# Rows of the experts' region in DRAM: 576 bytes apart in place of 528

## The chip, the cores and the metric

The kernel runs on one core of one Trainium2 chip. The metric is the time of one execution on the device in microseconds (us), the median of several runs. A core has five engines with an instruction stream each: TensorE (PE; its weight loads are listed as PEld), VectorE (DVE), ScalarE (ACT), GpSimd (POOL) and SyncE (SP), which here only issues DMAs. Sixteen DMA engines move data between DRAM and the on-chip memory.

## The reference

256 images of 128 channels and 7 x 7 places (12544 tokens of 128 numbers) pass four layers: window attention with a layer norm, a group-norm attention, and then twice an attention followed by a mixture of experts. The mixtures are what the change touches:

```python
scores = jnp.einsum('bne,ex->bnx', x, Wg) + bg
topk_vals, topk_idx = jax.lax.top_k(scores, TOP_K)      # TOP_K = 2 of 8 experts
gates = jax.nn.softmax(topk_vals, axis=-1)
h = jax.nn.gelu(jnp.einsum('bne,xeh->bnxh', x, W1) + b1, approximate=False)
expert_out = jnp.einsum('bnxh,xhe->bnxe', h, W2) + b2
out = jnp.einsum('bnx,bnxe->bne', combine, expert_out)  # combine: the two gates at the two experts
```

The second mixture has the same form with a hidden size of 512 in place of 192 and the tanh form of gelu. All numbers are fp32.

## The kernel before

The program runs stages one after another, with a barrier of all engines between two: window attention, group-norm attention, **dispatch 2** (the token attention of layer 2, and the sorting of tokens by expert), **blocks 2** (the experts' products), a combination of the two results of each token, **dispatch 3** (the attention of layer 3, and again the sorting), **blocks 3**, and a final combination with the store. The same class `Dispatch` sorts in both dispatch stages.

**The region.** `expert_rows` is a tensor in DRAM of 8 x 13312 + 512 rows, 13312 rows for each expert and 512 spare ones. A row is one token for one expert: its 128 normalised numbers (C = 128), then four more: the token's number (column C), its first expert (C + 1), and its two gates (C + 2, C + 3). A row is so 132 numbers, 528 bytes, and rows lie without a gap.

**Dispatch.** Tokens go in 98 tiles of 128, in chunks of 4 tiles (`CHUNKS_D2`, 25 chunks) or 3 (`CHUNKS_D3`, 33). A chunk's rows are put together in one of three tiles `row` (`NR = 3`): ACT writes the normalised numbers (L1375) and the first two columns (L1396, L1398), DVE the gates (L1497, L1499). DVE computes for each token the two places in the region (`pos`), and `scatter` on POOL sends each tile of 128 rows twice, one indirect DMA (L1565) for each of the two experts: 2 x 98 DMAs in a stage. At the start of the stage DVE runs `prepare`, which waits for eight loads of constants (L1405 and after), the last of them `d_pad` (L1258), a tile of 4 x 128 empty rows. When the places of all tokens are known, SP runs `pads`: it puts 512 empty rows behind the last token of each of the eight experts (L1277), waits for all of them (L1281), and the stage ends.

**Blocks.** `blocks_phase` goes over 56 blocks of 512 rows. For block b SP issues the load of the rows, `moe_xb<-expert_rows` (L2524), and then that of the expert's weights, `moe_w<-moe_split` (L2528). Three blocks can be loaded ahead; before the load of rows SP waits until the rows of block b-3 have been used (L2522), and before that of weights until the output `ys` of block b-3 is there (L2527). SP's queue is in order, so the rows of block b+1 are issued after the weights of block b. PE turns the 4 x 128 rows (L2539), multiplies by the first weights in chunks of the hidden size (L2551 to L2553; K is 2 chunks in blocks 2 and 4 in blocks 3), and by the second ones two chunks later (L2563 to L2565). POOL sends the results, rows of 128 numbers, 512 bytes, to `expert_out` (L2688, four indirect DMAs for each block).

The load of rows is one DMA whose destination is a tile of 128 partitions x 4 rows; in the trace it is 512 packets of one row, 32 on each of the 16 DMA engines. The empty rows are written in packets of one row in the same way.

Of the kernel before, what the change touches and what calls it, by code (L numbers as in the profile page):

```python
# [23 lines left out]
C = 128  # L24
# [19 lines left out]
REGION = 13 * 1024  # L44
assert REGION >= TOKENS + BLOCK
NBLK = (2 * TOKENS + EXPERTS * (BLOCK - 1)) // BLOCK
ROW = C + 4
FAR = 4.0 * TOKENS
EXP_SET = "natural_log_exp_and_others"

# [1135 lines left out]
class Dispatch:  # L1186
# [7 lines left out]
    def __init__(self, nc, sh, sb, sem, kind, e, wsplit, rows_dram, chunks, xt, small, joint=False):  # L1194
# [12 lines left out]
        self.upto8, self.steps, self.blocks = sb("upto8", [C, EXPERTS * EXPERTS]), sb("steps", [C, STEPS]), sb("blocks", [C, NBLK])  # L1207
        self.pad = sb("pad", [C, BLOCK // C, ROW])
        self.raw = [sb(f"raw{i}", [C, e.half]) for i in range(2)]
        self.wh, self.wl = [sb(f"wh{i}", [C, e.half], F32R) for i in range(2)], [sb(f"wl{i}", [C, e.half]) for i in range(2)]  # L1210
        self.st, self.mv = sb("dst", [C, QUAD, 6]), [sb(f"mv{i}", [C, QUAD, 2]) for i in range(2)]
        self.rs = [sb(f"drs{i}", [C, self.wide]) for i in range(2)]
        self.row = [sb(f"row{i}", [C, self.wide, ROW]) for i in range(self.NR)]
        self.lg = sb("lg", [C, self.wide, EXPERTS])
# [69 lines left out]

    def centre_gate(self, pe):
        pe.matmul(self.small[:, 0:EXPERTS], self.sh.centre_w[:, :], self.wg[:, :], start=True, stop=True).then_inc(self.centred, 1)
        pe.wait_ge(self.ready, 6)

    def turn(self, pe, q):
        c, t0, nt, o = self.quads[q]  # L1290
# [111 lines left out]
    def prepare(self, dve):  # L1402
        dve.memset(self.count[0][:, :], 0.0).then_inc(self.count_done, 1)
        dve.memset(self.base16[:, :], 0.0).then_inc(self.ready, 1)
        dve.wait_ge(self.loaded, 16 * 8)  # L1405
        dve.wait_ge(self.ready, 1)
        dve.tensor_copy(self.base16[0:1, :], self.base8[0:1, :]).then_inc(self.ready, 1)
        dve.tensor_copy(self.below[:, :], self.below_f[:, :]).then_inc(self.ready, 1)
        dve.tensor_copy(self.ones[:, :], self.ones_f[:, :]).then_inc(self.ready, 1)
        dve.wait_ge(self.centred, 1)  # L1410
        dve.tensor_copy(self.wgc[:, C:], self.small[:, 0:EXPERTS]).then_inc(self.ready, 1)
        dve.tensor_copy(self.wgc[:, 0:C], self.sh.centre_w[:, :]).then_inc(self.ready, 1)
# [143 lines left out]

    def scatter(self, pool, c, tiles=None):
        nt, j = self.chunks[c][1], c % self.NR
        pool.wait_ge(self.pos_done, c + 1)
        pool.wait_ge(self.normed, self.last_quad[c] + 1)  # L1560
        pool.wait_ge(self.col_done, c + 1)
        pool.wait_ge(self.named, 2 * c + 2)
        for i in range(nt) if tiles is None else tiles:
            for k in range(2):
                pool.indirect_dma_start(out=self.rows_dram, out_offset=bass.IndirectOffsetOnAxis(ap=self.pos[j][:, i, k:k + 1], axis=0),  # L1565
                                        in_=self.row[j][:, i, :], in_offset=None).then_inc(self.scattered[j], 16)
# [898 lines left out]
def blocks_phase(nc, sh, kind, e, func, wsplit, rows_dram, y_dram):  # L2465
# [8 lines left out]
    with ExitStack() as ctx:  # L2474
        def sb(name, shape, dt=F32):
            return ctx.enter_context(nc.sbuf_tensor(f"{kind}_{name}", shape, dt))
# [11 lines left out]
        w = [sb(f"w{i}", [C, e.width], F32R) for i in range(NW)]  # L2488
        xb = [sb(f"xb{i}", [C, S, ROW]) for i in range(NX)]
        xh, xl = [sb(f"xh{i}", [C, BLOCK], F32R) for i in range(2)], [sb(f"xl{i}", [C, BLOCK], F32R) for i in range(2)]  # L2490
# [329 lines left out]
def build(nc, a, out):  # L2820

    sh = Shared()
    sh.inputs = a
    rows_dram = nc.dram_tensor("expert_rows", (EXPERTS * REGION + BLOCK, ROW), F32, kind="Internal").ap()
    y_dram = nc.dram_tensor("expert_out", (2 * TOKENS, C), F32, kind="Internal").ap()
# [37 lines left out]
def constants():  # L2863
# [15 lines left out]
    one["c_blocks"] = np.tile(np.arange(NBLK, dtype=f), (C, 1))  # L2879
    pad = np.zeros((C, BLOCK // C, ROW), f)  # L2880
    pad[:, :, C] = FAR
# [51 lines left out]
```

## Time and profile before

| | |
|---|---|
| three runs | 2543.06, 2551.14, 2556.58 us; median 2551.14 |
| the profiled execution | 2569.39 us, its span 2567.6 us |
| busy: PE, DVE, ACT, POOL | 1885.7, 1682.2, 1394.9, 1398.4 us |
| DMA | 233.59 MB, 169830 packets |
| granted TensorE clock, mean | 0.836 |

The profile shows one execution of the program. Busy times are those of instructions that compute; an engine's idle time is put down to what ended it, an engine with a line or a DMA. The share of DMA is the mean over the 16 DMA engines. The profiled execution took 0.7% longer than the median of the three runs.

### The profile page before, as it was taken

Reading aid. Unit: us, or ns where it says so; the run is one execution under the profiler, and the core shown is the slowest. Engines: PE = TensorE matmul, PEld = TensorE weight load, DVE = VectorE, ACT = ScalarE, POOL = GpSimd, SP = SyncE. Lnnn points to the kernel's source line nnn. Section 1 sums busy time; section 2 is a strip of 40 time slices with the busy share of each in tenths; the row PEclk is TensorE's granted clock in tenths of the full one; section 3 lists DMA queues with packets and bytes.
Section 4 is the critical chain, followed back from the end, with each engine's and each line's share of the span. In section 5 each row is a group of like instructions: output and inputs, shape, how many; then the busy total and the mean of one; then the engine's idle time right before and its main releaser. Section 6 shows DMA issues by size and latency. Waiting matters only on the chain. (4 is left out here: it accounts for less than half of the span.)

```text
span 2567.6 us, 52818 instructions
## 1 busy us (share of the span) xinstructions
PE 1885.7 (73%) x16257; PEld 1299.3 (51%) x16257; DVE 1682.2 (66%) x4786; ACT 1394.9 (54%) x3150; POOL 1398.4 (54%) x1485
## 2 busy tenths in 40 slices
PE   7999998986546561677767478777777629999993
PEld 4555556764434451445544334444444427777772
DVE  5888886865434442455555458888888637887773
ACT  5777764645333431444444067777777417777760
POOL 4555560102434345356556637878787736776665
PEclk9999998988766755788888578979888659999995
DMA  5000000002101001555544511111110036777757
GB/s 115 3 0 0 0 1 1 0 16 81 51 29 35 26 33 57 151 146 147 142 137 136 209 21 66 51 47 52 47 62 25 29 122 214 227 230 230 228 170 300
DMA packets 169830, 233.59 MB, mean 91 GB/s; under 512 B 60032, under 2 KB 131957, under 8 KB 162190
## 3 DMA queue, kind: packets, MB, share of 16 engines
q1 hardware_dynamic: 142446, 172.32, 22.4%
q0 software_dynamic: 26880, 52.27, 6.1%
q10 hardware_dynamic: 288, 6.42, 0.6%
q8 instruction: 99, 1.62, 0.3%
q14 instruction: 117, 0.96, 0.1%
HBM read 155.37 MB, written 79.23 MB: 91 GB/s over the span
## 5 line engine op out<-in xcount | busy, mean ns | idle before, releaser
L2688 POOL DMA_INDIRECT expert_out<-moe_yr,moe_to x448 | 475.4, 1061 | 341.7 <-DVE moe_yr L2667 223.9
L1565 POOL DMA_INDIRECT expert_rows<-d_row,d_pos x392 | 381.1, 972 | 355.7 <-issue 163.5
L2603 ACT ACTIVATE moe_ah<-moe_hps,moe_w 128x512 f32<-128x512 f32 (+1 forms) x336 | 229.9, 684 | 256.5 <-PE moe_hps L2553 181.0
L2644 DVE TENSOR_TENSOR moe_hl<-moe_ah,moe_hh 128x512 fp32r<-128x512 f32 (+1 forms) x336 | 232.9, 698 | 171.4 <-ACT moe_hh L2608 108.9
L1782 PE MATMUL scales_ptps<-ident,scales_pr 113*128 113x113 f32 x512 | 110.0, 319 | 124.1 <-DVE scales_sc L1880 81.7
L2551 PE MATMUL moe_hps<-moe_xh,moe_w 128*128 128x512 f32 (+1 forms) x336 | 142.4, 424 | 48.3 <-DMA moe_w<-moe_split 32.4
L550 POOL TENSOR_TENSOR window_pr<-window_pr,window_rc 113x392 f32<-113x392 f32 x128 | 109.1, 852 | 106.8 <-DVE window_rc L494 106.7
L1782 PEld LDWEIGHTS scales_ptps<-ident,scales_pr 113*128 113x128 f32 x512 | 67.9, 163 | 179.2 <-DVE scales_sc L1880 95.3
L2563 PE MATMUL moe_yps<-moe_hh,moe_w 128*128 128x512 f32 (+1 forms) x336 | 152.5, 454 | 2.7 <-issue 0.9
L2539 PE MATMUL moe_xps<-ident,moe_xb 128*128 128x128 f32 x448 | 79.3, 306 | 95.5 <-DMA moe_xb<-expert_rows 91.1
L2564 PE MATMUL moe_yps<-moe_hl,moe_w 128*128 128x512 f32 (+1 forms) x336 | 138.7, 413 | 0.0
L2565 PE MATMUL moe_yps<-moe_hh,moe_w 128*128 128x512 f32 (+1 forms) x336 | 138.4, 412 | 0.0
L2552 PE MATMUL moe_hps<-moe_xl,moe_w 128*128 128x512 f32 (+1 forms) x336 | 137.8, 410 | 0.0
L2553 PE MATMUL moe_hps<-moe_xh,moe_w 128*128 128x512 f32 (+1 forms) x336 | 137.3, 409 | 0.0
L538 POOL TENSOR_TENSOR window_sc<-window_sc,window_mx 113x392 f32<-113x392 f32 x128 | 108.0, 844 | 50.2 <-DVE window_mx L468 49.3
L2539 PEld LDWEIGHTS moe_xps<-ident,moe_xb 128*128 128x128 f32 x448 | 58.6, 155 | 126.6 <-DMA moe_xb<-expert_rows 110.3
L2633 DVE TENSOR_TENSOR moe_xl<-moe_xps,moe_xh 128x512 fp32r<-128x512 f32 x112 | 76.5, 683 | 69.4 <-ACT moe_xh L2596 60.1
L2294 PE MATMUL d_turn<-ident,d_xn 128*128 128x128 f32 x128 | 28.0, 359 | 124.8 <-issue 93.7
L657 ACT ACTIVATE window_pt<-window_ptps 128x452 f32<-128x452 f32 x128 | 69.8, 546 | 90.0 <-PE window_ptps L334 89.9
L2011 POOL TENSOR_TENSOR scales_pr<-scales_pr,scales_fac 113x416 f32<-113x416 f32 x128 | 114.1, 904 | 3.9 <-DVE scales_fac L1918 2.5
L2139 ACT ACTIVATE scales_pt<-scales_ptps 128x452 f32<-128x452 f32 x128 | 69.9, 546 | 83.2 <-PE scales_ptps L1782 83.0
L2608 ACT ACTIVATE moe_hh<-moe_ah 128x512 fp32r<-128x512 f32 (+1 forms) x168 | 106.1, 632 | 5.3
(290 smaller groups left out, 5391.8 us busy)
## 6 DMA issues: line engine op xcount, KB each, us to landing
moe_w<-moe_split SPq DMA_DIRECT2D x56, 1026.5 KB
moe_xb<-expert_rows SPq DMA_DIRECT2D x112, 264.0 KB
moe_w<-moe_split SPq DMA_DIRECT2D x56, 449.5 KB
c_yy<-expert_out SPq DMA_DIRECT2D x28, 448.0 KB
final_yy<-expert_out SPq DMA_DIRECT2D x28, 448.0 KB
expert_out<-moe_yr,moe_to POOLq DMA_INDIRECT x448
X<-in_x SPq DMA_DIRECT2D x32, 196.0 KB
expert_rows<-d_row,d_pos POOLq DMA_INDIRECT x392
```

Of the source, the lines that this page charges most:

```text
L1565: pool.indirect_dma_start(out=self.rows_dram, out_offset=bass.IndirectOffsetOnAxis(ap=self.pos[j][:, i, k:k + 1], axis=0), in_=self.row[j] ...
L1782: last = pe.transpose(ptps[:, hp * R:(hp + 1) * R], pr[at.r][p][:, 2 * hp:2 * hp + 2, :].rearrange("q h k -> q (h k)"), ident[0:R, 0:R])
L2539: last = pe.transpose(xps[:, t * C:(t + 1) * C], xb[b % NX][:, t, 0:C], ident[:, :])
L2551: pe.matmul(out, ww[:, W1H + k * P:W1H + (k + 1) * P], xh[j][:, :], start=True, stop=False)
L2552: pe.matmul(out, ww[:, W1H + k * P:W1H + (k + 1) * P], xl[j][:, :], start=False, stop=False)
L2553: pe.matmul(out, ww[:, W1L + k * P:W1L + (k + 1) * P], xh[j][:, :], start=False, stop=True).then_inc(h_mm, 1)
L2563: pe.matmul(out, ww[0:P, W2H + k * C:W2H + (k + 1) * C], high, start=(k == 0), stop=False)
L2564: pe.matmul(out, ww[0:P, W2H + k * C:W2H + (k + 1) * C], low, start=False, stop=False)
L2565: pe.matmul(out, ww[0:P, W2L + k * C:W2L + (k + 1) * C], high, start=False, stop=(k == K - 1)).then_inc(y_mm, 1)
L2603: act.activation(ah[n % NH][0:P, :], hps[n % 3][0:P, :], func, bias=bias(b, k)[0:P]).then_inc(h_done, 1)
L2644: dve.tensor_tensor(hl[n % NH][0:P, :], ah[n % NH][0:P, :], hh[n % NH][0:P, :].bitcast(F32), ALU.subtract).then_inc(hl_done, 1)
L2688: pool.indirect_dma_start(out=y_dram, out_offset=bass.IndirectOffsetOnAxis(ap=to[j][:, t:t + 1], axis=0), in_=yr[j][:, t, :], in_offset=No ...
```

## The change

`ROW` is 144 in place of 132. Rows of the region, the tiles `row`, `pad` and `xb`, and the constant `c_pad` get 12 more numbers behind the four columns, so each of their transfers grows by one eleventh; a row now starts at a multiple of 576 = 9 x 64 bytes, where it started at a multiple of 528 = 33 x 16 bytes. Nothing reads the 12 numbers. As `scatter` sends whole rows, DVE sets them to zero once for each of the three tiles `row`, and three waits are adapted; `scatter` gets one wait more, once for each chunk.

```diff
-ROW = C + 4
+ROW = C + 16
...
     def centre_gate(self, pe):
         pe.matmul(self.small[:, 0:EXPERTS], self.sh.centre_w[:, :], self.wg[:, :], start=True, stop=True).then_inc(self.centred, 1)
-        pe.wait_ge(self.ready, 6)
+        pe.wait_ge(self.ready, 6 + self.NR)
...
     def prepare(self, dve):
         dve.memset(self.count[0][:, :], 0.0).then_inc(self.count_done, 1)
         dve.memset(self.base16[:, :], 0.0).then_inc(self.ready, 1)
+        for row in self.row:
+            dve.memset(row[:, :, C + 4:], 0.0).then_inc(self.ready, 1)
         dve.wait_ge(self.loaded, 16 * 8)
-        dve.wait_ge(self.ready, 1)
+        dve.wait_ge(self.ready, 1 + self.NR)
...
     def scatter(self, pool, c, tiles=None):
         nt, j = self.chunks[c][1], c % self.NR
+        pool.wait_ge(self.ready, 1 + self.NR)
         pool.wait_ge(self.pos_done, c + 1)
```

The only instructions that are added are on DVE, at the start of each dispatch stage. This is DVE's order there in dispatch 2 before (a row is line, operation, output<-input, size):

```order
L2330 MEMSET d_pt 128x392
L1403 MEMSET d_count 128x4
L1404 MEMSET d_base 128x4
L1407 CAST d_base<-d_base 1x8
L1408 CAST d_below<-d_below_f 128x128
```

And this is the same place of the changed kernel, whose lines below L1404 have moved by two and below the scatter by three:

```order
L2333 MEMSET d_pt 128x392
L1403 MEMSET d_count 128x4
L1404 MEMSET d_base 128x4
L1406 MEMSET d_row 128x4x12 x3
L1409 CAST d_base<-d_base 1x8
L1410 CAST d_below<-d_below_f 128x128
```

Three small memsets stand ahead of the cast that waits for the constants; nothing else has moved on any engine.

## Rows read from the trace of the kernel before

**Rows 1.** Busy us (instructions) of each engine by stage, clock, DMA
```profile
590.00:1037.00 447.00, 218.61 (x1549) 175.59 (x1547) 191.86 (x1047) 150.25 (x523) 188.38 (x196) 0.68 0.15 47
1036.00:1412.00 376.00, 269.78 (x1106) 189.98 (x1106) 201.76 (x497) 171.56 (x278) 212.53 (x213) 0.83 0.51 144
1488.00:2104.00 616.00, 431.81 (x5219) 260.59 (x5217) 479.07 (x1509) 414.66 (x1005) 434.56 (x491) 0.80 0.14 46
2104.00:2500.00 396.00, 378.28 (x1788) 296.65 (x1788) 300.12 (x671) 277.74 (x449) 245.79 (x219) 0.99 0.70 221
```
**Rows 2.** Waits in blocks 2 (1036 to 1412): us, times, longest
```profile
PE moe_xps L2539 <- DMA moe_xb<-expert_rows: 70.7, 33, 34.2
PE moe_hps L2551 <- DMA moe_w<-moe_split: 29.7, 25, 2.2
```
**Rows 3.** The same two waits in blocks 3 (2104 to 2503)
```profile
PE moe_xps L2539 <- DMA moe_xb<-expert_rows: 20.4, 1, 20.4
PE moe_hps L2551 <- DMA moe_w<-moe_split: 2.7, 1, 2.7
```
**Rows 4.** Timeline in blocks 2: start us, us, instruction [idle before]
```profile
1236.65 0.34 SPq L2528 DMA_DIRECT2D moe_w<-moe_split  x1
1238.87 0.00 SPq L2524 DMA_DIRECT2D moe_xb<-expert_rows  x1
1240.12 0.47 PE L2551 MATMUL moe_hps<-moe_xh,moe_w 128*96 128x512 f32 x1 [1.34 <-DMA moe_w<-moe_split]
1241.91 0.90 PE L2539 MATMUL moe_xps<-ident,moe_xb 128*128 128x128 f32 x3 [0.86 <-DMA moe_xb<-expert_rows]
```
**Rows 5.** Timeline, end of dispatch 2, and SP's wait for the pads
```profile
1007.61 24.15 SPq L1277 DMA_DIRECT2D expert_rows<-d_pad  x8
...
1009.27 0.96 POOL L1565 DMA_INDIRECT expert_rows<-d_row,d_pos  x1 [0.30 <-issue]
1010.53 0.95 POOL L1565 DMA_INDIRECT expert_rows<-d_row,d_pos  x1 [0.31 <-issue]
1011.79 0.96 POOL L1565 DMA_INDIRECT expert_rows<-d_row,d_pos  x1 [0.30 <-issue]
...
1024.42 0.96 POOL L1565 DMA_INDIRECT expert_rows<-d_row,d_pos  x1 [0.30 <-issue]
...
SPq L1281 <- DMA expert_rows<-d_pad: 2.2, 1, 2.2
```
**Rows 6.** DMA queues (packets, MB, share of 16 engines): 1026:1034, 650:1000, 1060:1400, 2120:2480
```profile
q1 hardware_dynamic: 2112, 1.08, 44.9%
...
q0 software_dynamic: 5120, 10.82, 9.3%
...
q1 hardware_dynamic: 33625, 36.55, 40.2%
...
q1 hardware_dynamic: 34944, 68.72, 62.2%
```
**Rows 7.** Indirect DMAs on POOL, ns min/median/max: rows of 528 and of 512 bytes
```profile
L1565 POOL DMA_INDIRECT expert_rows<-d_row,d_pos x392: 952/959/1280, 621.7 to 2092.4; - x196
L2688 POOL DMA_INDIRECT expert_out<-moe_yr,moe_to x448: 980/984/1459, 1055.2 to 2508.0; - x150
```
**Rows 8.** DVE's start of dispatch 2 and of dispatch 3
```profile
565.64 0.06 DVE L1404 MEMSET d_base<- 128x4 uint32 x1
569.00 0.16 DVE L1407 CAST d_base<-d_base 1x8 bf16<-1x8 f32 x1 [3.29 <-DMA d_pad<-in_c_pad]
...
1472.39 0.11 DVE L1851 MEMSET scales_xn<- 128x24 f32 x2
...
1478.08 0.16 DVE L1407 CAST d_base<-d_base 1x8 bf16<-1x8 f32 x1 [5.31 <-DMA d_pad<-in_c_pad]
```

## The prediction

> **What bounds the kernel now.** I read three views. The windows by stage come first [rows 1]. In both dispatch stages the DMA engines are busy for about a seventh of the time (0.15 and 0.14), in blocks 2 for half (0.51), in blocks 3 for 0.70. In blocks 3 PE is busy 378.28 of 396 us: that stage goes at PE's pace. In blocks 2 it is busy 269.78 of 376, so something else is in the way there. The waits name it second: in blocks 2 PE waits 70.7 us for the rows of a block, 33 times, of which 34.2 are the one wait at the stage's start, and 29.7 us for weights [rows 2]. What is left, 70.7 - 34.2 = 36.5 us in 32 waits, is the only place where transfers of rows hold PE again and again. In blocks 3 there is one wait of each kind, the first block's [rows 3]. The timeline shows what such a wait is made of: SP issues the rows at 1238.87 and PE starts on them at 1241.91, 3.0 us later, having stood for 0.86 [rows 4]. The reader should see that these 3 us are mostly the way to DRAM and back, as the packets of a load take less than 1 us (below). Third, the ends of the dispatch stages. POOL issues its last scatter at 1024.42, but SP's eight pads go from 1007.61 to 1031.76 and it waits 2.2 us more for them [rows 5]. So the stage ends with a DMA of rows, not with the scatters.
>
> **What a packet of a row costs now.** Between 1026 and 1034 the hardware queue carries only pads: 2112 packets, 44.9% of 16 engines over 8 us, so 0.449 x 8 x 16 / 2112 = 27.2 ns for a packet of at most 528 bytes [rows 6]. For the price of 48 more bytes I take the two windows of the blocks stages, where packets differ mostly in size. Blocks 2: 0.402 x 340 x 16 = 2187 us for 33625 packets and 36.55 MB. Blocks 3: 0.622 x 360 x 16 = 3583 us for 34944 packets and 68.72 MB [rows 6]. With a cost for each packet and one for each byte, these two equations give 18.7 ns for a packet and 0.0426 ns for a byte (scale the first to 34944 packets: 2273 us and 37.98 MB; the difference is 1310 us for 30.74 MB). Hence 48 bytes cost 2.0 ns. The bounds: 0, if the transfer goes in units that both lengths fill alike, and 27.2 / 11 = 2.5 ns if all of a packet's time is in its bytes. A load of rows or a pad is 32 packets on each engine, 0.87 us now, so it gets 32 x 2.0 = 0.064 us longer (0 to 0.08).
>
> Does the start at a multiple of 64 bytes give something back? The rows of a pad start at multiples of 16 bytes, most of them off 64, and their mean of 27.2 ns is not above what the fit gives for 528 bytes anywhere in memory, 18.7 + 22.5 = 41 ns with the traffic of the stage in it. The fit cannot exclude that part of these 41 ns is alignment, so it stays as a rival. I take 0 as the gain.
>
> The Trainium skill, "DMA: Bandwidth & Descriptors", section "How a descriptor splits into AXI transactions", has a rule that bears on this: a transfer is cut at multiples of 256 bytes and counted in beats of 32, and one that starts off such a multiple pays for the bytes before its start too. By it 528 bytes at multiples of 16 would cost 17 to 24 beats, 20.5 in the mean (an estimate from that page), and 576 bytes at multiples of 64 cost 18 to 24, 21 in the mean. By the rule the change would then make a packet 2.4% dearer, 0.7 ns or 0.02 us a load, a third of what I take, and the sum below would be +0.8 us; no run here shows single packets by their start yet.
>
> **The change part by part**, against the profiled execution (span 2567.6, time 2569.39 us).
>
> 1. Loads of rows in blocks 2. Each of the 32 waits that are not the first can get 0.064 us longer: 2.0 us. At most all 56 blocks would feel 0.08 us, 4.5 us; at least 0, since a wait for rows is followed by one for weights in 25 cases and may be paid back there. I take 2.0, because PE stands at most of them [rows 2].
> 2. Loads of rows in blocks 3: no wait but the first [rows 3]. What hides them is PE, busy 378 of 396 us, and the three blocks ahead; the row traffic adds 56 x 0.064 = 3.6 us to DMA engines that are busy 277 us of 396. Without this cover it would cost these 3.6 us. Taken: 0.
> 3. The first load of each blocks stage, after which everything waits: 2 x 0.064 = 0.13 us.
> 4. The last pad of each dispatch stage, for which SP waits: 0.13 us. The seven pads ahead are spaced by SP's issue, 24.15 us for seven intervals and the last issue, so about 3.4 us apart, against 0.87 us of packets [rows 5, 6], so they hide their longer packets.
> 5. The scatters: 392 DMAs, each 16 packets of 8 rows. From 650 to 1000 us 5120 packets (half of them the 4-byte signal) take 0.093 x 350 x 16 = 521 us, 203 ns a packet of 8 rows with its signal [rows 6]. They grow to about 219 ns, while POOL issues one each 1.26 us (1009.27, 1010.53, 1011.79 [rows 5]). What sets that pace is POOL's own instruction, and it does not follow the row's length: median 959 ns for 528 bytes and 984 for 512 [rows 7]. Cost 0; without the cover the 16 ns a DMA would come to 196 x 0.016 = 3.1 us in each dispatch.
> 6. The extra wait of each chunk on POOL. Behind it is the scatter of the chunk, and for its landing the writers of the tile wait three chunks later. The value it waits for is reached at the start of the stage. The step from 1009.27 to 1010.53 is the one from a chunk to the next, with four waits in it already, and its idle time is 0.31 us, as inside a chunk, 0.30 [rows 5]. Cost 0; the bound is 0.01 us x 58 chunks = 0.6 us.
> 7. Three memsets on DVE, twice. The nearest row is two memsets of 24 numbers a partition in 0.11 us; three of 48 are about 0.2 to 0.3 us. They run where DVE then stands 3.29 and 5.31 us for the constants [rows 8]. Cost 0; uncovered they are 0.6 us in all. PE's wait for `ready` behind them ends with DVE's last copy, which has not moved.
> 8. The constant `d_pad`, the load that ends this standing, goes from 2112 to 2304 bytes a partition: 192 x 0.0426 = 8 ns for each of 8 packets on an engine, 2 x 0.065 = 0.13 us.
>
> Sum: 2.0 + 0.13 + 0.13 + 0.13 = +2.4 us, bounds 0 and 4.5 + 0.5 + 0.6 + 0.6 = 6.2 us. On 2569.39 that is +0.09%; on the median of 2551.14 it gives 2553.5 us. The three runs of before lie between 2543.06 and 2556.58, 0.5% apart: a difference of less than 0.5%, 12.8 us, cannot be told from none, and this scatter, not the sum, makes the forecast's own range: 2543 to 2564.
>
> **The rivals.**
>
> A, the forecast: extra bytes, nothing back, most of it hidden. 2553.5 us.
>
> B, alignment pays in the blocks stages. In favour: the fit's 41 ns against 27.2 in the quiet window leaves 14 ns a packet that contention or alignment may explain. If all 14 went, a load would be 32 x 14 = 0.45 us shorter, and 32 waits of blocks 2 (1.14 us each in the mean) would give 14.4 us: 2551.1 - 14.4 + 2.4 = 2539 us. Against: the pads, which have the same unaligned starts, show no such part. From 12.8 / 32 = 0.4 us a load on it counts as faster. If the waits for rows vanished altogether (36.5 us), the time would be 2515.
>
> C, the other side: the new pitch collides in DRAM. Rows of one partition in a load lie 128 x 576 = 73728 bytes apart, which is 9 x 8192, before 33 x 2048; the regions of two experts lie 117 x 65536 bytes apart, before 429 x 16384. If whatever spreads addresses over the memory's banks looks at those low bits, the 16 engines, which start together, meet in the same bank. If a packet took twice its 27.2 ns, a load would be 0.87 us longer: 32 x 0.87 = 28 us in blocks 2, 2579 us in all. It decides (over 12.8 us) from 0.4 us a load on, a packet of 40 ns in quiet. For it speaks only the arithmetic; against it, that 9 is odd and no row shows such a collision at 2048 or 16384.
>
> D, the clock. In blocks 2 the granted clock is 0.83 in the mean [rows 1]. A small shift of the stages can change where it falls. A mean 0.02 lower or higher stretches 269.78 us of PE by 2.4%, 6.5 us either way: 2547 or 2560, still within the same.
>
> E, the rule of the skill as written, an arithmetic of beats, is a smaller sum of the same sign, and its chance is in A's.
>
> **How the numbers follow.** A with D around it 0.86; B over 0.5% 0.06; C over 0.5%, with what I have not seen of its kind, 0.08. The predicted time is A's. A's own 2543 to 2564 holds some four fifths of its share; to have 8 in 10 of all, I widen it to 2541 to 2566. Faster 0.06, same 0.86, slower 0.08.
>
> **What would show it.** Right: in quiet stretches with pads alone a packet of 29 to 30 ns; POOL's indirect DMA at 959 ns and 1.26 us apart; the first waits of DVE at 3.3 and 5.3 us; waits for rows in blocks 2 of 36 to 40 us without the first; blocks 3 with no wait but the first. Wrong: a packet of pads under 27 ns or over 40, waits for rows in blocks 2 that fall by half (B) or grow by 15 us or more (C), or a change in a stage that touches no rows.

## The result, and the profile after

The changed kernel takes 2562.56 us in the median of 12 runs (2554.16 to 2576.49), the kernel before 2551.00 us in 12 runs beside them (2541.92 to 2564.1). The ratio is 1.0049, with a 95% interval of 1.0028 to 1.0070: slower by 11.6 us between the medians. (The ratio isn't the quotient of the two medians, which is 1.0045.) A second set of runs of both gave 1.0049 again (1.0026 to 1.0073). The forecast was 2553.5 us, and +2.4 us.

The profiled execution has a span of 2562.5 us, less than the 2567.6 of before: single executions of one program lie up to 22 us apart (2541.92 and 2564.10), so the two spans can't be compared. Stages are compared below over several profiles.

The windows by stage of the changed kernel, laid to the same places of the stages as [rows 1] (busy us and instructions of PE, PEld, DVE, ACT, POOL; clock; DMA share; GB/s):

```profile
585.00:1032.00 447.00, 219.69 (x1571) 176.89 (x1571) 193.72 (x1050) 151.88 (x530) 187.93 (x196) 0.69 0.15 50
1031.50:1407.50 376.00, 268.58 (x1120) 188.72 (x1120) 203.09 (x504) 174.29 (x281) 222.98 (x222) 0.84 0.50 148
1472.00:2098.00 626.00, 432.69 (x5220) 262.44 (x5218) 478.86 (x1509) 414.01 (x1005) 433.85 (x491) 0.81 0.15 47
2098.00:2494.00 396.00, 379.25 (x1786) 297.72 (x1787) 303.06 (x670) 277.74 (x448) 248.95 (x218) 0.98 0.70 224
```

The DMA shares and the busy times are those of before; the largest move is POOL's in blocks 2, 222.98 us for 212.53, with 222 instructions in the window in place of 213. In blocks 2 PE has done 1120 matmuls after 376 us where it had done 1106: that stage isn't slower in this profile.

The waits of PE in blocks 2, then in blocks 3 of the changed kernel, which answer to [rows 2] and [rows 3]:

```profile
PE moe_xps L2542 <- DMA moe_xb<-expert_rows: 73.6, 33, 34.2
PE moe_hps L2554 <- DMA moe_w<-moe_split: 24.0, 18, 2.3
...
PE moe_xps L2542 <- DMA moe_xb<-expert_rows: 20.5, 1, 20.5
PE moe_hps L2554 <- DMA moe_w<-moe_split: 3.4, 1, 3.4
```

Without the first wait the rows now hold PE for 39.4 us in place of 36.5, and the weights for 24.0 in place of 29.7. Neither difference can be put down to the change. The same two rows, over windows of 376 us laid to the same place, of null (the kernel before once more) and of after2 (the changed kernel once more), two of the runs below:

```profile
PE moe_xps L2539 <- DMA moe_xb<-expert_rows: 71.2, 30, 34.3
PE moe_hps L2551 <- DMA moe_w<-moe_split: 32.8, 24, 2.2
...
PE moe_xps L2542 <- DMA moe_xb<-expert_rows: 75.5, 36, 34.3
PE moe_hps L2554 <- DMA moe_w<-moe_split: 30.6, 24, 2.4
```

The kernels with 528-byte rows in layer 2 have 36.5 to 46.8 us of waits for rows without the first (the 46.8 is sbuf_only's), so 2.9 us more is inside what they differ by among themselves.

The hardware queue of the changed kernel from 1021 to 1029 us, where it carries pads alone, and the indirect DMAs of POOL, answering to [rows 6] and [rows 7]:

```profile
q1 hardware_dynamic: 1853, 1.03, 42.6%
...
L1568 POOL DMA_INDIRECT expert_rows<-d_row,d_pos x392: 952/958/1142, 620.3 to 2086.8; - x196
L2691 POOL DMA_INDIRECT expert_out<-moe_yr,moe_to x448: 980/983/1482, 1051.3 to 2503.3; - x150
```

A packet takes 0.426 x 8 x 16 / 1853 = 29.4 ns against 27.2, 2.2 ns more. Both means count the short signal packets as well. POOL's instruction takes what it took, 958 ns.

DVE's start of dispatch 2, and the end of the stage on SP, answering to [rows 8] and [rows 5]:

```profile
565.21 0.21 DVE L1406 MEMSET d_row<- 128x48 f32 x3
568.66 0.16 DVE L1409 CAST d_base<-d_base 1x8 bf16<-1x8 f32 x1 [3.24 <-DMA d_pad<-in_c_pad]
```

```profile
1003.10 23.87 SPq L1277 DMA_DIRECT2D expert_rows<-d_pad  x8
...
SPq L1281 <- DMA expert_rows<-d_pad: 2.0, 1, 2.0
```

The three memsets take 0.21 us and lie in DVE's standing, which is 3.24 us where it was 3.29. The pads take 23.87 us (24.15) and the wait for them 2.0 (2.2).

What has moved is dispatch 3. It is measured from the start of SP's load of `d_below_f` in it to the start of SP's first load of rows in blocks 3. Timeline of SP in the kernel before, then in the changed kernel:

```profile
1471.76 0.33 SPq L1257 DMA_DIRECT2D d_below_f<-in_c_below  x1
...
2105.37 0.41 SPq L2524 DMA_DIRECT2D moe_xb<-expert_rows  x1
```

```profile
1456.27 0.33 SPq L1257 DMA_DIRECT2D d_below_f<-in_c_below  x1
...
2099.38 0.41 SPq L2527 DMA_DIRECT2D moe_xb<-expert_rows  x1
```

633.6 us before, 643.1 after: +9.5 us in a stage for which the forecast had given 0.13 (half of its terms 4 and 8). POOL computes for 439.95 us of the stage before and 439.24 after, so what grew is its idle time. The wait that grew is POOL's for ACT, at the start of its product `wf` (before, then after; us, times, longest):

```profile
POOL scales_wf L2002 <- ACT scales_rc L2131: 49.1, 32, 3.6
```

```profile
POOL scales_wf L2005 <- ACT scales_rc L2134: 60.6, 32, 3.7
```

It comes once in each of the 32 steps of the stage, and has grown by 11.5 us. One profile can't tell whether the stage differs or the execution; the experiments are made for that.

### The profile page after: what moved, and what is told of

The parts are those of the page before. It is cut to its first block and busy times, and to the rows that moved or that the text cites. A ratio compares the mean times of both kernels' runs of the same rounds, so it can differ in the third digit from the quotient of the medians.

```text
span 2562.5 us, 52824 instructions
## 1 busy us (share of the span) xinstructions
PE 1882.8 (73%) x16257; PEld 1299.2 (51%) x16257; DVE 1685.2 (66%) x4792; ACT 1394.6 (54%) x3150; POOL 1402.9 (55%) x1485
## 5 line engine op out<-in xcount | busy, mean ns | idle before, releaser
L2691 POOL DMA_INDIRECT expert_out<-moe_yr,moe_to x448 | 481.4, 1075 | 325.1 <-DVE moe_yr L2670 202.3
```

The costliest lines, as they stand in the source:

```text
L2691: pool.indirect_dma_start(out=y_dram, out_offset=bass.IndirectOffsetOnAxis(ap=to[j][:, t:t + 1], axis=0), in_=yr[j][:, t, :], in_offset=No ...
```

## The experiments

Every kernel ran 11 or 12 times, beside 12 to 35 runs of the kernel before. The experiments ran on four chips, which are not equally fast: the kernel before has medians of 2551.03 (chip 0), 2551.96 (chip 15), 2559.52 (chip 13) and 2563.66 us (chip 14). Each ratio compares runs of one chip, but the stage times, from one profile of each kernel, come from different chips. Dispatch 3 and blocks 3 (to the first load of the last stage) and the wait of POOL for ACT at `wf` are in the table for all kernels. For the profiles of before and of the change no chip is on record.

| kernel | row, bytes | extra waits | chip | ratio, 95% interval | dispatch 3, us | wait at `wf`, us | blocks 3, us |
|---|---|---|---|---|---|---|---|
| before | 528 | none | | | 633.6 | 49.1 | 406.4 |
| null | 528 | none | 15 | 0.9999 (0.9976 to 1.0022) | 636.5 | 51.1 | 407.2 |
| sbuf_only | 528 (tiles of 576) | none | 0 | 0.9991 (0.9966 to 1.0016) | 627.6 | 42.9 | 408.0 |
| w_only | 528 | one a call | 13 | 1.0028 (1.0006 to 1.0050) | 639.3 | 52.7 | 407.4 |
| w_four | 528 | four a call | 13 | 1.0053 (1.0032 to 1.0074) | 644.9 | 54.9 | 408.5 |
| w_sixteen | 528 | sixteen a call | 15 | 1.0063 (1.0042 to 1.0085) | 641.4 | 52.4 | 406.7 |
| the change | 576 | one a call | | 1.0049 (1.0028 to 1.0070) | 643.1 | 60.6 | 407.8 |
| after2, the same | 576 | one a call | 15 | 1.0049 (1.0026 to 1.0073) | 640.2 | 56.5 | 408.4 |
| d3_only | 528, layer 3: 576 | one a call, layer 3 | 0 | 1.0022 (0.9998 to 1.0046) | 643.4 | 57.9 | 407.3 |
| w_once | 576 | one a stage | 13 | 1.0035 (1.0014 to 1.0057) | 642.9 | 58.6 | 408.9 |
| r560 | 560 | one a stage | 14 | 1.0020 (0.9994 to 1.0046) | 640.2 | 60.6 | 408.5 |
| r592 | 592 | one a stage | 14 | 1.0009 (0.9985 to 1.0033) | 632.1 | 46.9 | 408.8 |
| w_once640 | 640 | one a stage | 13 | 1.0015 (0.9993 to 1.0037) | 630.4 | 42.7 | 408.9 |
| r1024 | 1024 | one a stage | 15 | 1.0026 (1.0000 to 1.0052) | 634.5 | 47.0 | 409.6 |

The expectations below, written before each run, name the possible causes as theories with a letter; these letters are not those of the prediction's rivals.

### Is it the wait of scatter?

In dispatch 3 `scatter` is called for each of the 98 tiles, with the products of the attention between the calls, so the change put 25 + 98 = 123 waits on POOL's queue and not the 58 of the forecast. In w_once they are taken back to one a stage:

```diff
-        pool.wait_ge(self.ready, 1 + self.NR)
+        if c == 0 and (tiles is None or 0 in tiles):
+            pool.wait_ge(self.ready, 1 + self.NR)
```

> The changed kernel with the extra wait of scatter kept only ahead of the first scatter of each dispatch stage. In dispatch 3 scatter is called once for each tile, so the change put 25 + 98 = 123 extra waits on POOL's queue, not 58. Theory W (the extra waits cost about 0.1 us each where POOL is waited for, 98 x 0.1 = 10 us in dispatch 3): back to 1.000 to 1.001 of the time before. Theory B (the longer rows cost it): unchanged, 1.004 to 1.005.

Measured: 1.0035, dispatch 3 at 642.9 us, between the two expectations and nearer to theory B. The stage did not come back; the total may have by 0.14% or by nothing, as the intervals overlap. So, by this one profile, dispatch 3 is slow with the longer rows even without the waits.

w_only is the reverse, the kernel before with one wait:

```diff
+        pool.wait_ge(self.ready, 1)
         pool.wait_ge(self.pos_done, c + 1)
```

> The kernel before with one more wait that is always fulfilled ahead of each call of scatter, rows of 528 bytes. Theory W: 1.004 to 1.005 of the time before, the growth in dispatch 3. Theory B: 1.000, within 0.2%.

Measured: 1.0028, dispatch 3 at 639.3 us, again between the two. So 123 waits that are always fulfilled cost 7 us (0.28%, from 0.06 to 0.50), though no step of POOL in the quiet end of dispatch 2 is longer for them: the steps from one scatter to the next stay at 1.26 us across a chunk too, even with sixteen waits.

w_four has four of them, on `ready`, `centred`, `loaded` and `count_done`, each at a value reached long before:

> The kernel before with four more waits, on four semaphores that are long fulfilled, ahead of each call of scatter. Theory W: four times the effect of one, 1.015 to 1.02. Theory B: 1.000, within 0.2%.

Measured: 1.0053, dispatch 3 at 644.9 us: less than twice the one wait, not four times. w_sixteen has sixteen, behind the wait for `pos_done`:

> The kernel before with sixteen more waits, all long fulfilled, ahead of each call of scatter, rows of 528 bytes. If a wait costs POOL time (one gave 1.0028, four 1.0053): 1.01 to 1.02, in dispatch 3 (98 x 16 waits; at 0.02 us each 31 us of POOL, not all on the path). If those two were only another rhythm: 1.002 to 1.006.

Measured: 1.0063, dispatch 3 at 641.4 us. So 1, 4 and 16 waits give +0.28, +0.53 and +0.63%. If each took time on the path, sixteen would give 4.5% by the first; the loss levels off instead. Of the two forms of the expectation the first (1.01 to 1.02) fell. The second (1.002 to 1.006) holds within the interval, 1.0042 to 1.0085.

The traces show a part of it directly. POOL's idle time just before the first scatter of a tile in dispatch 3 is 165 ns in the median before, with one wait and with four, and 306 ns with sixteen. Summed over all 196 scatters of the stage this idle time is 76.4 and 78.5 us in before and null, and 81.4, 83.2 and 84.3 with one, four and sixteen waits: 3 to 8 us more. In the changed kernel and after2 it is 78.8 and 78.6.

### Is it the bytes?

w_once with `ROW = C + 32`, rows of 640 bytes:

> Rows of 640 bytes, also a multiple of 64, with the extra wait only ahead of the first scatter of a stage: 112 bytes more than before in place of 48. Theory W: by the 0.0426 ns a byte, 32 waits x 0.15 us = +5 us, 1.002. Theory B (11.5 us for 48 bytes): 112 / 48 of it, +27 us, 1.0105.

Measured: 1.0015, dispatch 3 at 630.4 us. More bytes, and no more loss than 576: w_once, on the same chip, has 1.0035, with intervals that overlap. With `ROW = C + 128`, rows of 1024 bytes:

> Rows of 1024 bytes, with the extra wait only ahead of the first scatter of a stage: 496 bytes more than before, ten times the 48 of the change. If bytes on the wait for rows are what the change costs: by 0.0426 ns a byte 21.1 ns a packet, 0.68 us a load, 32 to 56 loads of blocks 2: +22 to +38 us, 1.009 to 1.015, nearly all in blocks 2. If the measured 11.5 us of 48 bytes were all bytes: +119 us, 1.047. If bytes are hidden: 1.002 to 1.004, as the other edits.

Measured: 1.0026, interval 1.0000 to 1.0052, dispatch 3 at 634.5 us, blocks 3 at 409.6. The first branch of the expectation, 1.009 to 1.015, fell too; the last, 1.002 to 1.004, holds. The waits of PE of this kernel in blocks 2:

```profile
PE moe_xps L2543 <- DMA moe_xb<-expert_rows: 101.9, 44, 35.5
PE moe_hps L2555 <- DMA moe_w<-moe_split: 18.4, 18, 1.6
```

The rows do hold PE for longer: 101.9 - 35.5 = 66.4 us without the first wait, 29.9 more than before, within what was expected of the waits (22 to 38). But blocks 2, from its first load of rows to the first load of the stage behind it, took 383.7 us in this profile, against 381.9 in that of null on the same chip (393.4 in the first profile of before). The longer waits for rows were nearly all absorbed: those for weights fell from null's 32.8 to 18.4 us, and the stage is held by something that isn't the sum of the two. So ten times the bytes cost that stage 1.8 us in this pair of profiles.

### Do two equal programs differ, and does the result hold?

null is the kernel before, after2 the changed kernel, both word for word.

> The kernel before once more under another name, unchanged. It shows how far two equal programs come apart, and how much the stages of one program differ from one profiled execution to the next. Every theory: 1.000, interval around it. Theory R (dispatch 3 runs in one of two rhythms, 633 or 643 us, and which one is decided anew in each execution): dispatch 3 anywhere between 630 and 645 us. Theory P (the rhythm belongs to the program): 633.6 us again, within 2 us.

> The changed kernel once more, unchanged. If the first result holds: 1.003 to 1.007. Theory P: dispatch 3 takes 643 us again, within 2 us. Theory R: anywhere between 630 and 645 us, and the ratio may come out as low as 1.002.

Measured: 0.9999 and 1.0049. Dispatch 3 of null, from the timeline of SP:

```profile
1447.32 0.33 SPq L1257 DMA_DIRECT2D d_below_f<-in_c_below  x1
...
2083.82 0.41 SPq L2524 DMA_DIRECT2D moe_xb<-expert_rows  x1
```

and of after2:

```profile
1454.48 0.33 SPq L1257 DMA_DIRECT2D d_below_f<-in_c_below  x1
...
2094.71 0.41 SPq L2527 DMA_DIRECT2D moe_xb<-expert_rows  x1
```

636.5 and 640.2 us: each 3 us off its first profile (633.6, 643.1), outside the 2 us that theory P allowed. So P falls as it was worded, and these two profiles, 3.7 us apart, leave theory R standing. Against R speaks the whole table: on each of the four chips every kernel with 560 or 576 bytes or a wait a call has a longer dispatch 3 than every other kernel there (640.2 and 641.4 against 634.5 and 636.5 on chip 15, 639.3 to 644.9 against 630.4 on chip 13, 640.2 against 632.1 on chip 14, 643.4 against 627.6 on chip 0).

Blocks 2 moves far more: 393.4 and 381.9 us in the two profiles of the kernel before. Over all profiles with a known chip it follows the chip and not the kernel: 376 to 384 us on chips 0 and 15, 385 to 393 on chips 13 and 14. A difference in blocks 2 or dispatch 2 below some 10 us can't be read from profiles of different chips. In blocks 3 one of 2 us can't either: w_four, whose edit is in the dispatch stages alone, has 408.5 us there against 406.4 and 407.2.

### Is it the tiles on the chip, and which layer?

sbuf_only has the tiles of the change (144 numbers wide, everything behind them at its addresses) and moves the 132 numbers of before:

```diff
+WIDE = C + 16
...
-        self.row = [sb(f"row{i}", [C, self.wide, ROW]) for i in range(self.NR)]
+        self.row = [sb(f"row{i}", [C, self.wide, WIDE]) for i in range(self.NR)]
...
-                                        in_=self.row[j][:, i, :], in_offset=None).then_inc(self.scattered[j], 16)
+                                        in_=self.row[j][:, i, 0:ROW], in_offset=None).then_inc(self.scattered[j], 16)
```

> On-chip tiles row, pad and xb as in the changed kernel (144 numbers wide, so all tiles behind them lie at its addresses), but every transfer moves the 132 numbers of before, and the region's rows are 528 bytes apart; no memsets, no extra wait. Theory S (the addresses of the tiles cost it): 1.003 to 1.005, dispatch 3 near 642 us. Theory D (the rows in DRAM and their packets, or the instructions added, cost it): 1.000, within 0.2%, dispatch 3 at 633 to 637 us.

Measured: 0.9991. Its dispatch 3 (timeline of SP) and POOL's wait for ACT in it:

```profile
1444.25 0.33 SPq L1258 DMA_DIRECT2D d_below_f<-in_c_below  x1
...
2071.84 0.41 SPq L2525 DMA_DIRECT2D moe_xb<-expert_rows  x1
```

```profile
POOL scales_wf L2003 <- ACT scales_rc L2132: 42.9, 32, 3.6
```

627.6 us, the shortest of all. Theory S falls, by the total and by this stage: the addresses and widths of the tiles aren't it. What is left is what theory D names, the rows that are moved or the instructions added.

d3_only has 576 bytes in layer 3 and 528 in layer 2, with two regions:

```diff
-ROW = C + 16
+ROW2, ROW3 = C + 4, C + 16
...
-        scales_dispatch_phase(nc, sh, scales, "d3", MOE3, w3, rows_dram)
+        scales_dispatch_phase(nc, sh, scales, "d3", MOE3, w3, rows3_dram)
```

> The change in layer 3 alone: dispatch 3 and blocks 3 with rows of 576 bytes in a region of their own, memsets and the extra wait for each tile; layer 2 as before. If dispatch 3 and blocks 3 hold the loss, as the profiles have it (643.1 and 640.2 us against 633.6 and 636.5 in dispatch 3, some 2 us more in blocks 3): 1.003 to 1.0045. If it lies in layer 2: 1.000 to 1.001.

Measured: 1.0022, interval 0.9998 to 1.0046, between the two expectations, with an interval that reaches into both. Its dispatch 3:

```profile
1444.68 0.33 SPq L1260 DMA_DIRECT2D d_below_f<-in_c_below  x1
...
2088.05 0.41 SPq L2532 DMA_DIRECT2D moe_xb<-expert_rows  x1
```

643.4 us: the stage is slow again, with layer 2 as before, and by 15.8 us against sbuf_only on the same chip. The rest of the loss, 0.27% by the two ratios, would lie in layer 2, but the interval also allows that there is none.

### Is 576 special?

Up to 576 bytes the scatters' packets carry 8 rows; from 592 on they carry fewer. The software queue from 98 to 415 us into dispatch 3 (packets, MB, share), before and after:

```profile
q0 software_dynamic: 3456, 7.31, 7.4%
```

```profile
q0 software_dynamic: 3392, 7.82, 7.8%
```

and with rows of 592 bytes:

```profile
q0 software_dynamic: 5280, 8.34, 8.5%
```

Half of the first two counts are signals of 4 bytes, so a packet has 7.31 MB / 1728 = 4230 bytes and 7.82 MB / 1696 = 4611 bytes, 8 rows. With 592 bytes the queue has half as many packets again. The packets' sizes in the trace say how the 8 rows that an engine gets of a scatter are cut: 4144 and 592 bytes for rows of 592 (7 rows and 1), 4480 and 640 for rows of 640 (7 and 1), twice 4096 for rows of 1024 (4 and 4), and 4224, 4480 and 4608 in one for rows of 528, 560 and 576. In all six a packet ends with the row that brings it to 4096 bytes or more.

Both kernels are w_once with another `ROW`, C + 12 and C + 20.

> Rows of 560 bytes, not a multiple of 64, with the extra wait only ahead of the first scatter; the scatters' packets hold 8 rows, 4480 bytes. Theory N (576 bytes is special, by its packets of 4608 bytes, the longest of all the sizes tried): dispatch 3 at 630 to 637 us, 1.001 to 1.002. Theory G (any growth short of 640, where the packets hold 7 rows, puts dispatch 3 into its slower rhythm): dispatch 3 at 640 to 644 us, 1.003 to 1.005. If a start off 64 bytes cost anything, this would be slower than the 576 bytes with the same wait, 1.0035.

> Rows of 592 bytes, not a multiple of 64, with the extra wait only ahead of the first scatter. Theory N: packets of 7 rows, 4144 bytes, dispatch 3 at 630 to 637 us, 1.001 to 1.002. Theory G, if packets of 7 rows are what spares 640: the same; if it is the row's length alone: 640 to 644 us, 1.003 to 1.005.

Measured: 1.0020 and 1.0009, with wide overlap (the quotients of the medians, 1.0007 and 1.0018, lie the other way round). Dispatch 3 of r560, then of r592, from the timeline of SP:

```profile
1469.52 0.33 SPq L1257 DMA_DIRECT2D d_below_f<-in_c_below  x1
...
2109.66 0.41 SPq L2528 DMA_DIRECT2D moe_xb<-expert_rows  x1
```

```profile
1471.49 0.33 SPq L1257 DMA_DIRECT2D d_below_f<-in_c_below  x1
...
2103.55 0.41 SPq L2528 DMA_DIRECT2D moe_xb<-expert_rows  x1
```

640.2 and 632.1 us, and POOL's wait for ACT in them is 60.6 and 46.9 us:

```profile
POOL scales_wf L2006 <- ACT scales_rc L2135: 60.6, 32, 3.6
```

```profile
POOL scales_wf L2006 <- ACT scales_rc L2135: 46.9, 32, 3.7
```

Theory N, that 576 alone is special, is contradicted by the profile of r560, whose dispatch 3 and whose wait at `wf` are like those of 576. But its total, 1.0020, would fit both theories, and one profile that is 3.7 us above null's doesn't decide it. Of theory G the branch in which packets of fewer rows spare the stage fits. r560, w_once, r592, w_once640 and r1024 have the same instructions in the same order, and differ in sizes only. Those with 8 longer rows in a packet have dispatch 3 at 640.2 and 642.9 us and the wait at `wf` at 60.6 and 58.6, those with fewer 632.1, 630.4 and 634.5 us and 46.9, 42.7 and 47.0. The totals don't confirm it: r1024, with a short dispatch 3, has 1.0026, and r560, with a long one, 1.0020. A start off a multiple of 64 bytes shows no cost: r592, off it, has 1.0009, and 640 and 1024 bytes, on it, 1.0015 and 1.0026.

## Why the prediction was right, and where it wasn't

The time, 2562.56 us, lies in the range of 2541 to 2566, and the difference of 0.49% is just under the bound of 0.5% that was called the same; but it is clear of zero, and nearly five times the forecast of +2.4 us. It is also outside the bounds of the sum itself, 0 to 6.2 us; the price of 3.1 us a dispatch that step 5 gave for the case without cover was not among them. The range held because it was made from the scatter of the runs, and that the time fell into it is luck as far as the cause goes. The sign and most of the single readings were right, the sum was not.

**Packets.** 2.0 ns more were forecast, with 0 to 2.5 as bounds; 2.2 were measured. Nothing came back for the alignment, as taken. The slope of the two-window fit was good: for rows of 1024 bytes it gives 21.1 ns more than for 528, and the data packets between 10 and 1 us before blocks 2, where pads alone move, take 47.2 ns in r1024 and 27.7 in null, 19.5 more. Its 41 ns for a packet of 528 bytes under traffic was not tested. The rule of the Trainium skill, "DMA: Bandwidth & Descriptors", section "How a descriptor splits into AXI transactions", would have given 0.7 ns; the measurement decides for more, over windows that mix all starts. Nor do single packets follow it: the rule counts 17 to 24 beats for 528 bytes by their start, and nine in ten of the data packets in the window of [rows 6] with pads alone took 27 to 29 ns.

**Step 1, loads in blocks 2** (+2.0 us). The waits for rows grew by 2.9 us, close to the term, but that is chance: the kernels with 528 bytes in layer 2 differ by more than 10 us in these waits. What shows more is r1024: 29.5 us more of them than null on the same chip, and a stage 1.8 us longer. So the term should have been close to its lower bound, 0. The reason given for that bound, that the wait for weights pays it back, is what r1024 shows (18.4 us for null's 32.8).

**Steps 2, 3, 4, 7, 8** (0, 0.13, 0.13, 0, 0.13 us). The memsets lie in DVE's standing (0.21 us in 3.24, and in dispatch 3 in 5.17). Blocks 3 took 407.8 and 408.4 us, 1.3 more in the mean than before and null, with one wait of rows as before; 408.5 to 409.6 with the other lengths from 560 to 1024. But sbuf_only and w_four, with 528 bytes, took 408.0 and 408.5, so it isn't shown that the 0 was short.

**Steps 5 and 6, the scatters and their wait** (0, at most 0.6 us and 3.1 a dispatch) is where the prediction failed. It was argued from the end of dispatch 2, where POOL issues scatters back to back and nobody else needs it. The other stage was left out: in dispatch 3 each scatter sits between products of the attention on POOL, and `scatter` is called for each tile there, so even the count was wrong, 123 waits and not 58 (`scatter` gets one wait more for each call, not for each chunk). That stage took 643.1, 640.2, 642.9 and 643.4 us in the four kernels with 576 bytes, and 633.6, 636.5 and 627.6 in the three with 528 and no added wait: 642.4 against 632.6 in the mean, +9.8 us. That is most of the loss of the change, 11.6 us. That no other stage has a part in it isn't shown, as dispatch 2 and blocks 2 differ by 10 us and more between the profiles.

**The rivals.** B (alignment pays) is refuted by the total, which rose, and by the pads. C (a collision in DRAM) is not what happened: it would show in the packets of the pads and in the waits for rows, and neither moved by that much. D (the clock) can't account for the loss, as the ratio came out at 1.0049 twice, and the granted clock over the whole of dispatch 3 is 0.80 after and 0.79 before. Over all profiles it is 0.78 to 0.81 in the eight with 639 us and more, and 0.79 to 0.82 in the other six.

**What is open.** Why dispatch 3 is slower with 8 rows of 560 or 576 bytes in a packet isn't shown. POOL's own instruction takes the same time, and no row has an engine waiting for a scatter there. What the profiles show is where the time goes: in the five kernels that scatter such rows there, POOL waits 56.5 to 60.6 us for ACT at `wf`, in the other nine 42.7 to 54.9. The added waits alone do something else: they bring the stage to 639.3 to 644.9 us without a byte more, with a wait at `wf` of 52.4 to 54.9 us, only 1 to 4 above null's 51.1, and with the 3 to 8 us more of idle time before the scatters. So there are two different losses of similar size, and what ties the length of the rows to the wait at `wf` was only found by correlation, with one profile for most kernels. Also open is how the loss of the change divides between the waits (w_once: 0.14% less, within the intervals) and the rows, and whether layer 2 has a part (d3_only). A kernel that scatters 576 bytes in packets of other sizes, with the loads unchanged, was not tried.

## What to carry to other kernels

A transfer that is off the path is cheap to enlarge: ten times the added bytes cost 0.26% here (0 to 0.52). Rows may be padded for convenience, but a start at a multiple of 64 bytes brought nothing by itself. When an edit touches a helper, count its calls in every stage that uses it, and cost it in the stage where its engine is shared, not where the trace is easiest to read. And before a difference of half a per cent is explained from two profiles, run the same program twice, and on the same chip: here one stage differed by 11.5 us between two profiles of one program, and over the profiles whose chip is known its time went with the chip.

## What was not expected of the hardware

- A wait that is already fulfilled isn't free on POOL's queue in a busy stage: 123 of them cost 0.28% (0.06 to 0.50), sixteen times as many only 0.63%. Yet one or four ahead of a scatter leave POOL's median idle time there at 165 ns, and sixteen bring it to 306.
- The rows of an indirect scatter are cut into packets by their bytes: 8 rows up to 576 bytes, 7 and 1 at 592 and 640, 4 and 4 at 1024.
- The same program gave 381.9 and 393.4 us for blocks 2 in two profiles, while blocks 3, where PE is busy for 0.95 of the time, stayed within 406.4 to 407.2. The kernel before had medians 0.5% apart on four chips.
- While POOL issues indirect DMAs, SP's pads are 4 to 6 us apart and an issue takes 0.70 us; after POOL's last one at 1024.42 [rows 5] they are 1.15 us apart and an issue takes 0.37. A pad is under 1 us of packets. That it is not the rows' length that spaces the eight pads of dispatch 2 is shown by r1024, where they take 23.68 us with 1024 bytes against 24.15 with 528. That it is POOL's issuing is what the timelines show, and was not tried by itself. The pads on SP in the kernel before, the first four and the last two:

```profile
1007.61 0.70 SPq L1277 DMA_DIRECT2D expert_rows<-d_pad  x1
1012.60 0.69 SPq L1277 DMA_DIRECT2D expert_rows<-d_pad  x1
1016.90 0.69 SPq L1277 DMA_DIRECT2D expert_rows<-d_pad  x1
1023.25 0.70 SPq L1277 DMA_DIRECT2D expert_rows<-d_pad  x1
...
1030.23 0.37 SPq L1277 DMA_DIRECT2D expert_rows<-d_pad  x1
1031.38 0.37 SPq L1277 DMA_DIRECT2D expert_rows<-d_pad  x1
```
